# A dynamic 1x1 convolution on one core: opening and last chunk rearranged

## What is computed

```python
# x: (32, 512, 56, 56) f32; everything below per sample b
xg = group_norm(x, groups=32, eps=1e-5)          # 16 channels and 56*56 positions to a group
pooled = mean(xg, (2, 3))                        # (B, 512)
h = relu(bn(pooled @ fc_w.T))                    # (B, 32)
ch_att = sigmoid(h @ ch_w.T + ch_b)              # (B, 512), scales input channels
fl_att = sigmoid(h @ fl_w.T + fl_b)              # (B, 512), scales output channels
kn_att = softmax(h @ kn_w.T + kn_b, axis=1)      # (B, 4)
agg_w = einsum('bk,koc->boc', kn_att, weight)    # 4 kernels of 512x512, mixed for each sample
y = einsum('bchw,boc->bohw', xg * ch_att, agg_w) * fl_att
out = x + (y - bn_m) * (bn_g / sqrt(bn_v + eps)) + bn_b
```

## Time and profile before

| | before |
|---|---|
| median of three runs | 2108.76 us |
| the profiled execution | 2107.46 us |
| its span, first to last instruction | 2105.7 us |
| PE busy | 2047.6 us, 97% |
| DVE busy | 1909.7 us, 91% |
| ACT busy | 1726.7 us, 82% |
| mean granted clock of PE | 0.998 |

### The profile page before, as it was taken

The page is one execution under the profiler, slowest core; times in us unless marked ns, Lnnn a source line. Parts: engine busy times, 40 slices in busy tenths (PEclk is TensorE's granted clock), DMA queues, the critical chain, the costliest instruction groups (busy, mean ns, idle before and its releaser), DMA issues.

```text
span 2105.7 us, 33303 instructions
## 1 busy us (share of the span) xinstructions
PE 2047.6 (97%) x10820; PEld 1058.4 (50%) x10820; DVE 1909.7 (91%) x3079; ACT 1726.7 (82%) x2295; POOL 0.2 (0%) x4
## 2 busy tenths in 40 slices
PE   0999999999999999999999999999999999999998
PEld 0455555555555555555555555555555555555554
DVE  7999999999999999999999999999999999999973
ACT  4788888888888888888888888888888888888885
POOL 0000000000000000000000000000000000000000
PEclk9999999999999999999999999999999999999999
DMA  9465556565556565556655565665565655566522
GB/s 333 134 210 199 199 189 207 206 209 196 196 200 206 195 209 199 202 192 209 209 196 205 191 206 196 209 206 194 192 209 202 208 200 192 196 206 207 175 105 105
DMA packets 237284, 415.99 MB, mean 198 GB/s; under 512 B 7248, under 2 KB 236624, under 8 KB 236752
## 3 DMA queue, kind: packets, MB, share of 16 engines
q1 hardware_dynamic: 237264, 415.74, 57.8%
HBM read 210.19 MB, written 205.52 MB: 197 GB/s over the span
## 4 chain that ended last, share of the span: by engine, by line
PE 97%; DVE 1%; DMA 1%; ACT 1%; SPq 0%; issue 0%; DVEq 0%
PE product L696 32%; PE product L695 32%; PE product L697 32%; DMA x_ring<-x 1%; DVE mixed_weight L557 0%; PE small L668 0%; DVE chunk_stats L354 0%; SPq L198 0%; DVE w_lo L573 0%; ACT y L295 0%; ACT x_norm L232 0%; DVE x_lo L362 0%; ACT x_hi L241 0%; ACT w_hi L308 0%; DVE x_ring L368 0%
## 5 line engine op out<-in xcount | busy, mean ns | idle before, releaser
L695 PE MATMUL product<-x_hi,w_hi 128*128 128x448 f16 x3584 | 1264.7, 353 | 6.7 <-DVE x_lo L362 3.6
L696 PE MATMUL product<-x_lo,w_hi 128*128 128x448 f16 x3584 | 1264.8, 353 | 0.0
L697 PE MATMUL product<-x_hi,w_lo 128*128 128x448 f16 x3584 | 1264.5, 353 | 0.0
L250 ACT ACTIVATE y<-product,out_bias,out_scale 128x448 f32<-128x448 f32 x896 | 641.8, 716 | 260.6 <-PE product L697 254.8
L232 ACT ACTIVATE x_norm<-x_ring,norm_bias,norm_scale 128x448 f32<-128x448 f32 x896 | 671.0, 749 | 1.4 <-DVE norm_bias L435 1.4
L368 DVE TENSOR_TENSOR x_ring<-x_ring,y 128x896 f32<-128x896 f32 x448 | 480.7, 1084 | 92.0 <-ACT y L250 86.0
L695 PEld LDWEIGHTS product<-x_hi,w_hi 128*128 128x128 f16 x3584 | 353.5, 99 | 335.3 <-issue 10.5
L697 PEld LDWEIGHTS product<-x_hi,w_lo 128*128 128x128 f16 x3584 | 351.1, 98 | 328.2 <-issue 1.6
L696 PEld LDWEIGHTS product<-x_lo,w_hi 128*128 128x128 f16 x3584 | 351.0, 98 | 322.4 <-issue 1.3
L354 DVE BATCH_NORM_STATS2 chunk_stats<-x_ring 128x6 f32<-128x448 f32 x896 | 492.8, 613 | 3.7 <-DMA x_ring<-x 1.2
L362 DVE TENSOR_TENSOR x_lo<-x_norm,x_hi 128x1792 f16<-128x1792 f32 x224 | 451.8, 2017 | 13.1 <-ACT x_hi L241 11.4
(11 more groups left out here) (69 smaller groups left out, 257.6 us busy)
## 6 DMA issues: line engine op xcount, KB each, us to landing
x_ring<-x SPq DMA_DIRECT2D x224, 896.0 KB, 4.8
out<-x_ring SPq DMA_DIRECT2D x224, 896.0 KB, 3.9
weight<-wt SPq DMA_DIRECT2D x4, 1024.0 KB, 15.1
params<-par SPq DMA_DIRECT2D x1, 462.0 KB, 3.4
```

The source lines that it names most:

```text
L250: nc.scalar.activation(y[:, s % 2, t], acc[k % BANKS][:, 0:COLS], ACT.Identity, bias=obias[:, t:t + 1], scale=oscale[:, u, t:t + 1]).then_ ...
L695: nc.tensor.matmul(bank, whi[:, u, t, cols], hi, start=(t == 0), stop=False)
L696: nc.tensor.matmul(bank, whi[:, u, t, cols], lo, start=False, stop=False)
L697: ins = nc.tensor.matmul(bank, wlo[:, u, t, cols], hi, start=False, stop=(t == CT - 1))
```

## The change

Loads: the seven chunks of sample one come first, then `params`, then the weights as eight halves (two tiles of one kernel each), then the seven chunks of sample two.

Opening: the batch-norm constants (`v_all` to `obias`) move from DVE to Pool. DVE takes only the statistics of sample one. The absolute sums are taken by halves (`top(j)`) between `guess`, the first normalised tile and `exponentials`. ACT writes `xhi` of chunks 0 and 1 straight from `xs` (`first_hi`); chunk 0's parts lie in rooms that `whi[:, 1]`, `wlo[:, 1]` and `y[:, 1]` lend. DVE makes the f32 `xn` of chunk 0 (`first_norm`). ACT mixes kernel 0 for output tiles 1 to 3 (`mix_first`), DVE for tile 0; DVE adds the others by tile (`add_kernel`), with the weight scale's steps between them. PE (`first_products`) runs for seven banks the two products that need only `xhi`, eight matmuls each, then their `xlo` products, four each, then the eighth bank whole.

First turn: it is written out. The statistics of sample two's chunks 7 to 10 come at s = 0, those of the following ones at places of their own (`first_stats_at`), and the preparation of sample two stands about one chunk later (`early`). The additions of chunks 0 to 5 (`EARLY_ADDS` = 6) are done by DMAs that Pool issues, with `accum_op=ALU.add`, two tiles each; ACT's evictions two chunks on and SP's stores wait for these.

Last chunk: during chunk 12 of the last turn ACT adds the bias `obias` to chunk 13 in place, four passes. DVE then reads each bank of the last chunk, multiplies and adds to the ring in one SCALAR_TENSOR_TENSOR, and SP stores each of four blocks (224 KB) when it is done.

```diff
@@ sync
-            sp.dma_start(pa[:, :], par).then_inc(params_in, 16)
             for slot in range(RING):
-                if slot == CHUNKS + 2:
-                    for k in range(KERNELS):
-                        sp.dma_start(w[:, k], wt[:, k]).then_inc(weight_in[k], 16)
+                if slot == CHUNKS:
+                    sp.dma_start(pa[:, :], par).then_inc(params_in, 16)
+                    for j in range(2 * KERNELS):
+                        k, half = divmod(j, 2)
+                        two = slice(half * CT // 2, (half + 1) * CT // 2)
+                        sp.dma_start(w[:, k, two], wt[:, k, two]).then_inc(weight_in[j], 16)
...
+                    if first and s < EARLY_ADDS:
+                        for h in range(2):
+                            sp.wait_ge(half_in[h], 16 * (s + 1))
...
+            for t in range(CT):
+                sp.wait_ge(tail_done[t], 1)
+                sp.dma_start(out_d[B - 1, :, t, (CHUNKS - 1) * COLS:], xs[:, RING - 1, t]).then_inc(tail_out[t], 16)
@@ scalar
+                if first and s < 2 + EARLY_ADDS:
+                    if s >= 2 and t % 2 == 0:
+                        act.wait_ge(half_in[t // 2], 16 * (s - 1))
...
+            act.wait_ge(bn_vars_ready, 1)
+            nc.scalar.activation(ln_all[:, :], v_all[:, :], ACT.Ln).then_inc(bn_guess_ready, 1)
+            act.wait_ge(bn_guess_ready, 1)
+            nc.scalar.activation(r_all[:, :], ln_all[:, :], ACT.Exp, scale=-0.5).then_inc(bn_guess_ready, 1)
+            top(0)
+            top(1)
             guess(start, 0)
+            for j in range(2, 6):
+                top(j)
+            first_hi(0, 0)
+            exponentials(start, 0)
+            top(6)
+            top(7)
+            for t in range(1, CT):
+                first_hi(0, t)
+            mix_first(1)
+            weight_hi(0)
+            mix_first(2)
+            first_hi(1, 0)
+            first_hi(1, 1)
+            weight_hi(1)
+            first_hi(1, 2)
+            first_hi(1, 3)
+            mix_first(3)
+            weight_hi(2)
+            norm(start, 1, 0, True)
+            norm(start, 1, 1, True)
+            weight_hi(3)
+            norm(start, 1, 2, True)
+            norm(start, 1, 3, True)
             for t in range(CT):
+                norm(start, 2, t, True)
+            split(start, 2)
...
+                early = {"guess": (3, 3), "exp": (4, 2), "mix": (4, 2), "split": (5, 3)}
+                usual = {"guess": (3, 0), "exp": (4, 0), "mix": (4, 1), "split": (5, 2)}
...
+                        if last and s == RING - 2:
+                            nc.scalar.activation(xs[:, s + 1, t], xs[:, s + 1, t], ACT.Identity,
+                                                 bias=obias[:, t:t + 1]).then_inc(tail_biased, 1)
@@ vector
-            for t in range(CT):
-                stats(start, CHUNKS, t)
             group_var(start, 0)
-            stats(start, CHUNKS + 1, 0)
             norms(start, 0)
...
+            def first_norm(t):
+
+                nc.vector.tensor_scalar(xn0[:, t], xs[:, 0, t], nscale[:, 0, t:t + 1], nbias[:, 0, t:t + 1],
+                                        ALU.mult, ALU.add).then_inc(xn0_ready, 1)
+
+            dve.wait_ge(att_ready, 1)
+            for half in range(2):
+                dve.wait_ge(weight_in[half], 16)
+            step(nc.vector.tensor_scalar(mix[:, :, 0:P], w[:, 0, :, 0:P], katt[:, 0:1], None, ALU.mult))
+            add_kernel(0, 1)
+            dve.wait_ge(abs_done, 2 * KERNELS)
             nc.vector.reduce_sum(wsum1[:, :], wsum[:, :], AX.X).then_inc(wsum_ready, 1)
+            add_kernel(0, 2)
             dve.wait_ge(top_moved, 1)
             nc.vector.reduce_max(wtop[:, :], top_row, AX.X).then_inc(wtop_ready, 1)
+            add_kernel(0, 3)
             dve.wait_ge(top_moved, 2)
...
             scaled_attentions(start, 0).then_inc(catt_ready, 1)
+            add_kernel(1, 1)
             dve.wait_ge(catt_ready, 1)
+            first_split(0)
+            add_kernel(1, 2)
+            add_kernel(1, 3)
+            add_kernel(2, 1)
+            first_split(1)
+            add_kernel(2, 2)
+            add_kernel(2, 3)
+            add_kernel(3, 1)
+            first_split(2)
+            add_kernel(3, 2)
+            add_kernel(3, 3)
+            first_norm(0)
+            first_norm(1)
+            first_split(3)
+            first_norm(2)
+            first_norm(3)
+            dve.wait_ge(xn0_ready, CT)
+            dve.wait_ge(first_hi_ready, CT)
+            nc.vector.tensor_tensor(xlo0, xn0, xhi0, ALU.subtract).then_inc(lo_ready, 1)
...
+                whole = {(0, 0): 7, (0, 1): 8, (0, 2): 9, (0, 3): 10, (2, 2): 11, (2, 3): 12, (3, 0): 13,
+                         (6, 1): 14, (6, 2): 15, (6, 3): 16}
...
+                early = {"means": (3, 1), "mean": (3, 1), "var": (3, 1), "norms": (4, 0), "logits": (4, 2),
+                         "att": (4, 3), "mix": [(5, 0), (5, 1), (5, 2)], "split": {(6, 0): (0, 1, 2, 3)}}
...
+                for t in range(CT):
+                    k = CT * (RING - 1) + t
+                    dve.wait_ge(tail_biased, t + 1)
+                    dve.wait_ge(mm_done, turn.at(4 * RING, k + 1))
+                    nc.vector.scalar_tensor_tensor(out=xs[:, RING - 1, t], in0=acc[k % BANKS][:, 0:COLS],
+                                                   scalar=oscale[:, 1, t:t + 1], in1=xs[:, RING - 1, t],
+                                                   op0=ALU.mult, op1=ALU.add).then_inc(tail_done[t], 1)
@@ gpsimd
+            def add(s, half):
+
+
+                pool.wait_ge(evac_done, BANKS + 4 * s + 2 * half + 2)
+                if s:
+                    pool.wait_ge(half_in[half], 16 * s)
+                two = slice(2 * half, 2 * half + 2)
+                pool.dma_start(xs[:, s, two], y[:, s % 2, two], accum_op=ALU.add).then_inc(half_in[half], 16)
@@ tensor
+            def first_products():
+                for s, o in ((0, 0), (0, 1), (1, 0), (1, 1), (0, 2), (1, 2), (0, 3)):
+                    first_part(s, o, False)
+                for s, o in ((0, 0), (0, 1), (0, 2), (0, 3), (1, 0), (1, 1), (1, 2)):
+                    first_part(s, o, True)
+                first_part(1, 3, False)
+                first_part(1, 3, True)
```

More of the change, by code:

```diff
@@ L192, in build @@
         NORM_AHEAD, SPLIT_AHEAD = 2, 1
+        EARLY_ADDS = 6
         @block.sync
@@ new lines, in first_hi, with mix_first @@
+            def first_hi(s, t):
+                if s == 0 and t == 0:
+                    act.wait_ge(norm_ready, 1)
+                nc.scalar.activation(xhi0[:, t] if s == 0 else xhi[:, 1, t], xs[:, s, t], ACT.Identity,
+                                     bias=nbias[:, 0, t:t + 1], scale=nscale[:, 0, t:t + 1]).then_inc(first_hi_ready, 1)
+            def mix_first(o):
+                cols = slice(o * P, (o + 1) * P)
+                if o == 1:
+                    act.wait_ge(att_ready, 1)
+                nc.scalar.activation(mix[:, :, cols], w[:, 0, :, cols], ACT.Copy,
+                                     scale=katt[:, 0:1]).then_inc(first_mix0_ready, 1)
@@ L279, in _, with weight_hi @@
+            def weight_hi(o):
+                cols = slice(o * P, (o + 1) * P)
+                if o == 0:
+                    act.wait_ge(catt_ready, 1)
+                act.wait_ge(first_mix_ready, o + 1)
+                for t in range(CT):
+                    nc.scalar.activation(whi[:, 0, t, cols], mix[:, t, cols], ACT.Copy,
+                                         scale=catt[:, t:t + 1]).then_inc(first_whi_ready, 1)
             act.preload_act_table_set("natural_log_exp_and_others")
@@ L300, in _ @@
-            for t in range(CT):
[L301 to L311, removed]
+            act.sem_inc(ln_ready, 1)
@@ L624, in body @@
                     prepare = not (last and b == 2)
+                    at = early if first and b == 1 else usual
                     for t in range(CT):
-                        if t == 0 and s:
-                            if prepare and n == 2:
-                                stats_complete(turn, b)
+                        if (n, t) == (2, 0) and prepare and at is usual:
+                            stats_complete(turn, b)
+                        if t == 0 and s and not (first and s - 1 < EARLY_ADDS):
@@ L657, in body @@
                         assert done[0] - before == STEPS, done[0] - before
-                add(turn, RING - 1, 1)
-            with dve.Fori(0, TURNS - 1) as i:
+                if not last:
+                    add(turn, RING - 1, 1)
+                    return
+                for t in range(CT):
+                    k = CT * (RING - 1) + t
[4 more added lines that the diff above has]
+                                                   op0=ALU.mult, op1=ALU.add).then_inc(tail_done[t], 1)
@@ L706, in body @@
                         product(turn, s, o)
-                        if prepare and (n, o) == (3, 2):
```

(4 more changed lines are left out.)

259 lines of the change are left out of this document (152 added, 107 removed).

## The result

The changed kernel took 2104.89 us (median of 12 runs, 2100.4 to 2107.99), the kernel before 2107.77 beside it (12 runs, 2106.13 to 2108.95): ratio 0.9983, 95% interval 0.9975 to 0.9992. So it is faster, by 2.9 us, where I had forecast 16.8, and 2104.89 lies outside my range. The change ended within 0.2% of the kernel before, to which I had given a chance of 0.02. The profiled execution took 2105.93 us with a span of 2104.1.

What follows compares the result with a forecast made beforehand. PE, busy 97% of 2105.7 us, was taken as the bound. Opening 16.0, minus 2.2 for late DVE, plus 2.9 for the tail gave 16.7 us won, forecast 2092.0 us, range 2088.3 to 2098.5.

Steps and rivals of the forecast that it cites:

- Loads, attention, absolute sums: Opening: seventh chunk landed at 19.88, logits' end 30.8, `catt` 36.45, first product at 37.7 us, 12.3 earlier.
- GpSimd's steps: Opening, batch-norm constants on Pool: eight dependent steps have 0.79 us each before DVE needs `bn_ready` at 28.35; expected hidden.
- High passes: Opening, first products: `lo_ready` at 52.0, PE waits 1.4 us, chunk 2 starts at 59.6 against 75.59, gain 16.0.
- DVE late after chunk 2: First turn: new PE waits of 1.0 us at chunk 7 and 1.2 at chunk 8; booked -2.2, bounds 0 and -5.
- P: The start of chunk 2 on PE, from which the forecast counted later times in us.
- Additions by DMA, "Hidden": First turn, chunks 0 to 5: each 448 KB addition takes 2.6 to 7.8 us, 11 us a pair allowed; no loss.
- Rival 4: First turn: additions by DMA delay evictions two chunks on and become the bound, slower than before; chance 0.02.
- Rival 3: Pool delays, by steps over 0.79 us or starved descriptors, or DVE's backlog is 5 us: 2096 to 2102; chance 0.12.
- rival 1: The clock falls in short waits before low passes and at chunk 7 or 8: 2094.5 to 2096.5; chance 0.2.
- Tail: Last chunk: one DVE operation of 0.68 us and a 224 KB last store, gain 2.9 us, bounds 2.0 and 3.5.

Runs made afterwards that it cites:

- e3_half_bytes: The changed kernel, but each accumulating DMA adds one tile of its two, so work is left out; 2089.95 us, ratio 0.9913.
- e9: The changed kernel with DVE's statistics of chunks 14 to 23 and the preparation of sample three later in the first turn; 2096.67 us, ratio 0.9946.
- e1_pool_adds: The changed kernel with the twelve additions of chunks 0 to 5 as GpSimd instructions, not DMAs; 2098.43 us, ratio 0.9953.
- e5: The changed kernel, but in the first turn SP issues the store of slot s + 1 before waiting for that of slot s; 2101.35 us, ratio 0.9966.
- e11: The changed kernel with four chunks added by DMA, SP's next store issued ahead, and statistics of chunks 14 to 23 behind the splits; 2099.37 us, ratio 0.9958.

## Why the prediction was wrong

**Loads, attention, absolute sums: right.** 20.18 (19.88), the logits' end 31.1 (30.8), `catt` 36.3 (36.45), first product 37.39 (37.7). GpSimd's steps took 0.20 to 0.31 us, and `bn_ready` came at 24.6, well ahead of 28.35.

**High passes: right, 0.9 us too dear.** `first_norm` took 0.51 us, two of them 0.93 (0.5 each), `x_lo` of chunk 0 ended at 50.8 (52.0), PE waited 1.06 (1.4) and the clock stayed. Chunk 2 started at 58.43 (59.6), 0.3 of it from the earlier first product: 17.2 won, not 16.0. By the Trainium skill, "VectorE: DVE Perf Modes", section "The perf-mode tier table" (two elements a cycle), I had an estimate of 0.35 for each `first_norm`; the rows have 0.46 to 0.51, so it is the sum's 0.5 that came true.

**DVE late after chunk 2: right.** 1.35 and 0.97 us in `e3_half_bytes`, where nothing else disturbs them, against 1.0 and 1.2. The 1.0 rested on chunk 7 at 121.81; from its first matmul at 121.24 PE would be there at P + 45.65, and the same working gives 1.55.

**Additions by DMA, "Hidden": this step failed.** I named three that wait for an addition (ACT's eviction, PE behind it, SP's store) and asked of the store only whether chunk 14's reload comes before P + 43. I wrote down that "both operands read" would make 7.8 us, and then used it as time to landing alone. What an addition takes from others, I never summed: 2.3 us of all DMA engines each, 4.7 a chunk, on top of the 4.8 that stores and reloads take of 9.08. The reloads of chunks 17 to 21, not that of 14, came late, and through DVE's order (shown by `e9`) they cost 11.3 of the 12.2 us of waits (0.97 is chunk 8's own, as in `e3`) and 4.5 us of clock. In `e3` all of that is gone.

**Rival 4 had the right resource and the wrong victim.** It let the additions delay the evictions, with 11 us allowed for a pair. No eviction waited: an addition landed in 7.5 us (median), and both halves overlap. The sentence "they share the DMA engines with stores and loads" stood there and had no price. Rival 3's starved descriptors didn't show: GpSimd issued each addition in 0.85 to 1.03 us. Nor did rival 1: in `e3` the granted clock stayed at 1.00 through the waits of 1.02, 1.35 and 0.97.

**Tail: right.** 3.0 (2.9), alone and in the whole, with 0.68 us for DVE's operation as taken.

So without what that step missed 18.0 us are won (`e3`) where I had 16.7, and the measured terms add up to it, 17.2 - 2.3 + 3.0 = 17.9. With what it missed, 2.9 are won.

## What to carry to other kernels

Price a transfer twice: as time to landing for whoever waits for it, and as time of the DMA engines for every other transfer of the same stretch; then sum the second against the length of that stretch. Ask what a late reload stands in front of on an in-order engine, chunk by chunk and not only for the first. And before a queue's order is changed, list what each later item then waits for: a reload put behind the next slot's addition waited for an engine, not for a store.

## What the runs showed of the hardware

An accumulating DMA from SBUF to SBUF filled the DMA engines at 196 GB/s, half the rate of plain loads (387), so 448 KB cost 2.3 us of all of them. With two of these under way beside stores and loads a store landed in 12.7 us, against 7.6 in the same stretch of `e1_pool_adds` and 3.9 in the kernel before. A GpSimd addition of 128x896 f32 took 2.09 us alone, DVE's takes 1.08, and beside GpSimd a DVE mix took 4.1 instead of 2.35. The changed kernel scattered by 7.6 us between lowest and highest (12 runs) and `e5` by 8.5 (6), against 0.4 (5) for `e3` with half the bytes. The share alone doesn't explain it: `e11` stood at 1.01 in 75 to 100 us and scattered by 1.7, so the cause stays open.
